# Attention: q and k in two F32R parts, score products of two heads in the two halves of the array

## The reference

```
q, k, v = heads of einsum('btc,fc->btf', layernorm(x), w_qkv)
scores = einsum('bhqd,bhkd->bhqk', q, k) * hs ** -0.5
p = softplus(scores);  p = p * p;  p = p * causal
attn = p / (sum(p) + 1e-9)
x = x + einsum('btc,oc->bto', attn @ v, w_proj) + b_proj
```

## Time and profile before

| | |
|---|---|
| Median of 3 runs | 1591.7 us (1588.0 to 1592.0) |
| The profiled execution | 1588.5 us, its span 1586.4 us |
| Busy: TensorE | 1517.2 us, 96% |
| Busy: VectorE | 1197.2 us, 75% |
| Busy: ScalarE | 872.5 us, 55% |
| qkv phase | about 188 to 275 us of the span |
| attention phase | about 276 to 613 us of the span |
| DMA | mean 60 GB/s |

### The profile page before, as it was taken

The page is one execution under the profiler, slowest core; times in us unless marked ns, Lnnn a source line. Parts: engine busy times, 40 slices in busy tenths (PEclk is TensorE's granted clock), DMA queues, the critical chain, the costliest instruction groups (busy, mean ns, idle before and its releaser), DMA issues. The chain is left out here.

```text
span 1586.4 us, 29112 instructions
## 1 busy us (share of the span) xinstructions
PE 1517.2 (96%) x11188; PEld 1121.0 (71%) x11188; DVE 1197.2 (75%) x2482; ACT 872.5 (55%) x1372; POOL 354.0 (22%) x366
## 2 busy tenths in 40 slices
PE   8999897999999999999989999989999999899998
PEld 7888776444444446888877777766777777678777
DVE  4555697899989996655588887778777777678786
ACT  3333387999999996332332222288888887321220
POOL 0002111100000004000432222114555554211111
PEclk9999999999999999999999999999999999999999
DMA  4100065777777750000110000023333233100000
GB/s 152 34 1 14 4 190 185 102 108 108 108 102 103 101 73 1 14 1 1 40 34 1 1 1 1 3 68 107 97 107 101 97 101 104 41 14 27 14 27 27
DMA packets 57017, 95.80 MB, mean 60 GB/s; under 512 B 7760, under 2 KB 29488, under 8 KB 56880
## 3 DMA queue, kind: packets, MB, share of 16 engines
q1 hardware_dynamic: 55920, 93.35, 26.3%
q10 hardware_dynamic: 960, 0.59, 0.2%
HBM read 76.88 MB, written 17.04 MB: 59 GB/s over the span
## 5 line engine op out<-in xcount | busy, mean ns | idle before, releaser
L928 DVE SCALAR_TENSOR_TENSOR X<-ps,moe_gsel,X 128x256 f32<-128x256 f32 x512 | 246.1, 483 | 71.3 <-PE ps L48 48.5
L1440 DVE TENSOR_TENSOR att_weights<-att_weights 128x1024 f32<-128x1024 f32 (+1 forms) x240 | 263.7, 1148 | 35.6 <-ACT att_weights L1416 35.5
L1416 ACT ACTIVATE att_weights<-ps 128x1024 f32<-128x1024 f32 (+1 forms) x288 | 263.6, 990 | 27.4 <-PE ps L1349 14.6
L48 PE MATMUL ps<-w_experts_hi,moe_xh 128*128 128x512 f32 x512 | 204.2, 399 | 0.1
L48 PE MATMUL ps<-w_experts_hi,moe_xl 128*128 128x512 f32 x512 | 203.1, 397 | 0.0
L48 PE MATMUL ps<-w_experts_lo,moe_xh 128*128 128x512 f32 x512 | 201.5, 394 | 0.0
L1379 PE MATMUL ps<-att_weights,att_v_ones 64*32 64x64 f32 (+5 forms) x2048 | 157.6, 398 | 0.1
L424 ACT ACTIVATE ffn_gates<-ps,ffn_gate_bias 128x512 f32<-128x512 f32 x72 | 49.6, 689 | 148.2 <-PE ps L48 126.5
L48 PEld LDWEIGHTS ps<-w_experts_hi,moe_xh 128*128 128x128 f32 x512 | 96.1, 188 | 24.5 <-DVE X L928 0.7
L48 PEld LDWEIGHTS ps<-w_experts_lo,moe_xh 128*128 128x128 f32 x512 | 96.1, 188 | 22.2
L48 PEld LDWEIGHTS ps<-w_experts_hi,moe_xl 128*128 128x128 f32 x512 | 96.1, 188 | 20.9
(11 more groups left out here) (281 smaller groups left out, 3548.7 us busy)
## 6 DMA issues: line engine op xcount, KB each, us to landing
ssm_lb<-decays SPq DMA_DIRECT2D x32, 512.0 KB, 4.7
ssm_rise<-decays SPq DMA_DIRECT2D x28, 512.0 KB, 4.0
qk_parts<-qkv_part SPq DMA_DIRECT2D x32, 384.0 KB, 2.8
q_stack<-qk_parts SPq DMA_DIRECT2D x64, 128.0 KB, 4.6
k_stack<-qk_parts SPq DMA_DIRECT2D x64, 128.0 KB, 8.0
att_q_stack<-qk_parts SPq DMA_DIRECT2D x64, 128.0 KB, 4.8
att_k_stack<-qk_parts SPq DMA_DIRECT2D x64, 128.0 KB, 8.3
out<-X SPq DMA_DIRECT2D x7, 512.0 KB, 2.9
```

What stands on the lines that cost most here:

```text
L48: ins = pe.matmul(out, l(k), r(k), start=first and n == 0, stop=last and n == len(passes) - 1)
L928: dve.scalar_tensor_tensor(out=x, in0=ring[:, e // 2, (e % 2) * C:(e % 2 + 1) * C], scalar=gsel[:, s, j, e:e + 1], in1=x, op0=ALU.mult, op ...
L1416: act.activation(Wt[:, u % WU, 0:n], scores(u)[:, 0:n], ACT.Softplus).then_inc(softplus_done, 1)
L1440: dve.tensor_tensor(wt, wt, wt, ALU.mult).then_inc(sq_dve, 1)
```

## The change

q and k are written in two F32R parts (high and remainder), 512 KB a store. The second rounding, the third part and their buffers and semaphores go. A stack now has 64 rows for a head: four copies, all four products of two parts. Even heads of the four lie in the lower 64 rows, odd heads in the upper 64, and the free dimension holds two heads instead of four, in F32R: as many bytes as before, 16 DMAs of 128 KB a set, each row of DRAM now 4 KB. A score product reads 64 rows: the two heads of a unit use the two halves of the array and the two banks. Their order in a unit alternates between the heads, and the mask products of REST units follow in pairs, 64 rows each. An UPPER unit is spread over two banks of 256 columns; its products are plain f32 of 64 x 64 in the four quarters of the array, the mask product is made of four 256-column products. Softplus and square of it read 2 x 256 columns. Which heads share rows in the value step changes with it (`h // 2` for `h % 2`), the number of its products doesn't.

The core of the diff:

```diff
-PARTS = 3
-Q_PART = (0, 0, 0, 1, 1, 1, 2, 2)
-K_PART = (0, 1, 2, 0, 1, 2, 0, 1)
-COPIES = P // HD
-STACKED = [(q_or_k, n) for q_or_k in range(2) for n in range(COPIES)]
+PARTS = 2
+HALF = P // 2
+Q_PART = (0, 0, 1, 1)
+K_PART = (0, 1, 0, 1)
+COPIES = HALF // HD
+STACKED = [(q_or_k, odd, n) for q_or_k in range(2) for odd in range(2) for n in range(COPIES)]
...
-        part = sb("part", [P, HALVES, QK, PARTS, GN], BF16)
-        rest = sb("rest", [P, 2, GN], F32)
+        part = sb("part", [P, HALVES, QK, PARTS, GN], F32R)
...
-                    pe.wait_ge(rest_done, n * QK + u + 1)
+                    pe.wait_ge(part1_done, n * QK + u + 1)
...
-            def second(n, h, u):
-                act.wait_ge(rest_done, RING + n * QK + u + 1)
-                act.activation(part[:, h, u, 1], rest[:, u % 2], ACT.Copy).then_inc(part1_done, 1)
...
-            def third(n, h, u):
-                dve.wait_ge(part1_done, n * QK + u + 1)
-                dve.tensor_tensor(part[:, h, u, 2], rest[:, u % 2], part[:, h, u, 1], ALU.subtract).then_inc(part2_done, 1)
...
-                dve.wait_ge(part2_done, 1 + n * QK + max(0, u - 1))
-                dve.scalar_tensor_tensor(out=rest[:, u % 2], in0=ring[:, u], scalar=SCALE[u],
-                                         in1=part[:, h, u, 0], op0=ALU.mult, op1=ALU.subtract).then_inc(rest_done, 1)
+                dve.scalar_tensor_tensor(out=part[:, h, u, 1], in0=ring[:, u], scalar=SCALE[u],
+                                         in1=f32(part[:, h, u, 0]), op0=ALU.mult, op1=ALU.subtract).then_inc(part1_done, 1)
...
-                sp.wait_ge(part2_done, 1 + (i * HALVES + h) * QK + u + 1)
+                sp.wait_ge(part1_done, RING + (i * HALVES + h) * QK + u + 1)
...
-        eng.dma_start(stacks[q_or_k][s][n * HD:(n + 1) * HD],
-                      src.rearrange("(h d) t -> d h t", h=HG)).then_inc(loaded[s], 16)
+        at = odd * HALF + n * HD
+        eng.dma_start(f32(stacks[q_or_k][s][at:at + HD]),
+                      src.rearrange("(g o d) t -> o d g t", o=2, d=HD)[odd]).then_inc(loaded[s], 16)
...
-                pass_units.append([(2 * pair + t, kj, t, c, q, w, part) for t in range(2) for kj, c, q, w, part in together])
+                pass_units.append([(2 * pair + t, kj, t, c, q, w, part) for kj, c, q, w, part in together for t in range(2)])
...
-        uppers = [(h, first + j, 0, (j * 2 + h // 2) * HALF, (first + j) * P, HALF, UPPER) for j in range(GT) for h in range(HG)]
+        uppers = [(h, first + j, h % 2, j * HALF, (first + j) * P, HALF, UPPER) for j in range(GT) for h in range(HG)]
...
-                    for r in range(2):
-                        pe.matmul(scores(u)[r * HALF:(r + 1) * HALF, 0].rearrange("p (s q) -> p s q", q=HALF), neg[low, low],
-                                  ident16[low, low].unsqueeze(1).broadcast_to([HALF, BANK // HALF, HALF]), start=True, stop=False)
+                    for pair in range(2):
+                        for odd in range(2):
+                            own = halves[odd]
+                            pe.matmul(scores(u)[halves[pair], odd, 0:GT * HALF].rearrange("p (j q) -> p j q", q=HALF), neg[own, own],
+                                      ident16[own, own].unsqueeze(1).broadcast_to([HALF, GT, HALF]), start=True, stop=False)
...
-                    ins = pe.matmul(scores(u)[rows, t, c:c + w], SK[s][:, h, keys], SQ[s][:, h, q:q + w],
-                                    start=not upper, stop=n >= len(segments) - 2 if upper else part == FULL)
-                    if part == REST:
-                        ins = pe.matmul(scores(u)[:, t, c:c + HALF], neg[:, :], ident16[:, HALF:P], start=False, stop=True)
+                    own = halves[h % 2]
+                    if upper:
+                        ins = pe.matmul(scores(u)[halves[h // 2], t, c:c + w], f32(SK[s][own, h // 2, kj * P:kj * P + HALF]),
+                                        f32(SQ[s][own, h // 2, q:q + w]), start=False, stop=n >= len(segments) - HG)
+                        continue
+                    ins = pe.matmul(scores(u)[:, t, c:c + w], SK[s][own, h // 2, kj * P:(kj + 1) * P], SQ[s][own, h // 2, q:q + w],
+                                    start=True, stop=part == FULL)
+                    if part == REST and h % 2:
+                        for odd in range(2):
+                            own = halves[odd]
+                            ins = pe.matmul(scores(u)[:, odd, c:c + HALF], neg[own, P:2 * P], ident16[own, own], start=False, stop=True)
...
-                act.activation(Wt[:, u % WU, 0:n], scores(u)[:, 0:n], ACT.Softplus).then_inc(softplus_done, 1)
+                act.activation(Wt[:, u % WU, :, 0:w], scores(u)[:, :, 0:w], ACT.Softplus).then_inc(softplus_done, 1)
```

More of the change, by code:

```diff
@@ L1142, in step @@
                     norm.act_apply(act, n + 2, h, lambda j: tile_of(n + 2, j))
-                for u in range(QK - 2, QK):
-                    second(n, h, u)
                 if left >= 3:
@@ L1188, in step @@
                     tail.dve_add(dve, n + 3, 1 - h)
-                for u in range(QK - 2, QK):
-                    third(n, h, u)
-            dve.sem_inc(rest_done, RING)
-            dve.sem_inc(part2_done, 1)
+            dve.sem_inc(part1_done, RING)
             for h in range(HALVES):
@@ L1271, in attention_phase @@
         at = len(pass_units)
[L1272 removed]
+        uppers = [(h, first + j, h % 2, j * HALF, (first + j) * P, HALF, UPPER) for j in range(GT) for h in range(HG)]
         pass_units.append(uppers)
         pass_steps.append((qb, at, [(h, kj, at, t, c, q, w, part) for h, kj, t, c, q, w, part in uppers]))
[L1275 removed]
+    WIDTH = [BANK // 2 if unit[0][-1] == UPPER else BANK for unit in pass_units]
     PU, PS = len(pass_units), len(pass_steps)
@@ L1376, in value_step @@
                     q0 = q - qb * BANK
-                    rows = slice(h % 2 * HALF, (h % 2 + 1) * HALF) if part == UPPER else slice(0, P)
-                    values = va_up[rows, s, kj, h // 2] if part == UPPER and h % 2 else va[rows, s, kj, h]
+                    rows = halves[h // 2] if part == UPPER else slice(0, P)
+                    values = va_up[rows, s, kj, h % 2] if part == UPPER and h // 2 else va[rows, s, kj, h]
                     ins = pe.matmul(O(qb)[h * 2 * HD:(h + 1) * 2 * HD, q0:q0 + w], values,
@@ L2329, in build @@
                 assert not jobs
-                stacks = [[sides.enter_context(nc.sbuf_tensor(f"{x}_stack{n}", [P, HG, T], BF16, side="right"))] for x in "qk"]
+                stacks = [[sides.enter_context(nc.sbuf_tensor(f"{x}_stack{n}", [P, HG // 2, T], F32R, side="right"))] for x in "qk"]
                 loaded = [nc.alloc_semaphore(name=f"loaded{n}_{s}") for s in range(2)]
@@ L2363, in layout @@
     cols = lambda v: np.ascontiguousarray(v.reshape(-1, P).T)
+    masks = np.triu(np.full((P, P), -1e30, np.float32), 1)
     return {
@@ L2377, in layout @@
         "proj_b": d["L0_attn_b_proj"],
-        "masks": np.triu(np.full((P, P), -1e30, np.float32), 1),
+        "masks": np.concatenate([masks, np.tile(masks[P // 2:], (2, 1))], axis=1),
         "ssm_w": _rows(d["L1_attn_in_proj_w"].T),
```

33 lines of the change are left out of this document (12 added, 21 removed).

## The result

The changed kernel takes 1572.4 us (median of 4 runs, 1569.8 to 1573.1) against 1590.5 for the kernel before in the same job: a ratio of 0.989, 95% interval 0.988 to 0.990. Its profiled execution is 1572.0 us with a span of 1569.9. That is a gain of 18 us where 38 were forecast; it lies inside the range, between rivals B and D.

The account below looks back on a forecast made before the run. TensorE was taken to bound attention and VectorE the qkv stage; 1588.5 less 7 (qkv) and 29 (attention, 1.8 in each of 16 passes) gave 1552.5, stated as 1554 us beside the median, range 1543 to 1582.

Parts of the forecast that it names:

- rival B: Attention: TensorE still binds through loads in turn, slow narrow F32R or dear upper units; 1561 to 1570 us, chance 0.25.
- rival D: Attention: value steps wait on VectorE's lag where it squares all eight units; 1570 to 1586 us, chance 0.11.
- What bounds the kernel: TensorE sets the attention pass of 20.63 us; VectorE sets the qkv step of 10.84 us.
- qkv: qkv stage: removed copies and subtractions shorten a step to 9.5 us, saving 7 us in all; bounds 4 and 10.
- The loop over VectorE: qkv stage: residual, statistics, remainders, add and tanh, put at 8.8 us a step after the change.
- Do the halves overlap: Score products: the two 64-row halves of the array run together, so a full unit costs one product's time.
- C: Score units: the two row halves run one after the other, so the kernel gets slower; 1628 us, chance 0.11.
- Triangle units: Attention's triangle (REST) score units: 1.6 us a pass saved, bounds 0 and 2.1, taking F32R loads as mostly hidden.
- Full units: Attention's full score units: eight products at 0.238 us plus four switches, 2.3 instead of 3.9, 1.6 saved a pass.
- UPPER and transposes: UPPER units go from 0.70 to 0.75 us, 0.1 lost a pass; the transposes' extra switches cost 0.2 a pass.
- What is late next: Attention: ScalarE becomes the bound at 18.4 us a pass, plus 0.4 for its waits on score units: 18.8.
- the forecast's own case: Attention, case A: halves run together and ScalarE binds at 18.8 us a pass; 1548 to 1559 us, chance 0.53.

Follow-up runs that it names:

- The experiment: Changed kernel with a ScalarE copy and a VectorE subtraction of the old sizes put back into each qkv unit, results unread: 1579.2 us, ratio 0.993.
- late masks: Changed kernel with the four mask products of each triangle unit moved behind all its score products: 1561.0 us, ratio 0.982.
- bf16 halves: Changed kernel with the two parts, DRAM buffer and stacks in bf16 instead of F32R, upper products in bf16 too: 1545.2 us, ratio 0.972.
- heads in turn: Changed kernel with both products and masks of one head before the other head's in a triangle unit: 1573.8 us, ratio 0.990.
- F32R masks: Changed kernel with triangle units' mask products in F32R instead of bf16: 1577.5 us in the usual order, 1574.6 with masks behind all score products.
- the kernel without masks: Changed kernel without the mask products of the triangle units, run twice: 1577.4 us, then 1573.2 us.
- the early division: VectorE's division one unit earlier: kernel before 1588.9 us; changed kernel 1569.2 us; with masks behind all score products too, 1559.9 us.

## Why the prediction was right or wrong

**What bounds the kernel: right.** TensorE set the pass before, VectorE the qkv stage. The division, which could have been a hidden second bound of the pass before, cost nothing there (20.62 for 20.63).

**qkv: right in kind, some 2 us too small.** 7 us were forecast, with bounds 4 and 10. From its first product to its last the stage takes 74.7 us instead of 82.6, and with the 1.4 of the earlier last store that is 9.3. The experiment's 6.9 comes so near to the forecast because it leaves that store early. The step fell to 9.3 instead of 9.5, TensorE's floor, and stands there without an idle row. The loop over VectorE, put at 8.8, didn't bind.

**Do the halves overlap: right, and C is out.** Pairs start together, whatever the order of the heads.

**Triangle units: the step that failed most.** The term was 1.6 us a pass with bounds 0 and 2.1. By starts, the eight units with their switches take 4.59 us after the change (four single ones 0.60 each, two pairs 1.09) for 4.94 before: 0.35. The forecast took the upper half of the bounds because the loads of the value products, 16 in 1.01 us, hide altogether. That was the wrong row: those loads stand among products of 320 to 512 columns, while here every second F32R load of a unit stands behind a 64-column one, and the unit's first behind another shape or a mask. No row in front showed an F32R load behind a short product; the nearest price, at most 0.118 a load from the v products, had been worked out and set aside. The unit's two bare loads cost 0.10 (0.51 less the 0.41 of late masks) and 0.12 (0.41 less the 0.29 of bf16), near that bound: 0.29 and 0.22 are the 0.51 measured. The two loads of a pair run beside each other (both at 469.52), which is why it is not the 0.59 of loads in turn. The Trainium skill's rule that was weighed against the change (TensorE: Matmul & The Clock Gate, section on weight-path perf modes: the fast weight load needs a type other than FP32) came out right in effect: with bf16 weights and the same products in the same order, the unit takes 0.29.

**Full units: the second one.** The term was 1.6 saved; it is 0.84 (3.04 us for the eight units, four singly at 0.43 and two pairs at 0.66, for 3.88 before). The product itself is 0.23 as forecast (0.66 less 0.43), but each group of score units starts with a bare F32R load, six of them a pass, which the forecast counted at nothing. A single unit with its switch takes 0.44 here (459.27 to 459.71) and 0.32 with bf16 weights (442.44 to 442.76 in that kernel).

**UPPER and transposes: right.** 0.70 for 0.75, and 0.3 a pass for the switches of the transposes instead of 0.2.

**What is late next: wrong in kind.** 0.4 us a pass was left for ScalarE's ring. The pass got 0.42 on VectorE's division instead, rival D's kind of wait at a place that D didn't name; that the two figures agree is chance. In sum: 20.63 - 0.35 - 0.84 + 0.26 for the transposes + 0.42 = 20.12, and the other groups are 0.04 shorter; measured 20.08. TensorE's own work is then 19.7, the upper end of rival B (whose sum, 20.7 - 1.6 + 0.6, gives 19.7 and not the 19.9 that it states); B's time was too early by the wait.

**The sum.** Of the 16.5 us between the two profiled executions 9.8 are gained up to attention's first score product (0.4 of them in front of the qkv stage) and 7.4 in attention, less 0.7 behind. The forecast had 7 and 29: it failed in attention, and the 2 us more from qkv, which hide a little of that, are luck. The price of the forecast's own case was good: where the loads are fast (bf16 halves), ScalarE binds, with VectorE as full as it, and the pass of 18.63 and the time of 1545 stand beside 18.8 and 1548 to 1559. ScalarE's work is 18.5 us there for the counted 18.4, so nearly nothing of the 0.4 for waits was needed. What was mis-sized was the chance and the term of the F32R load, not the mechanism.

## What to carry to other kernels

Before counting a product by its columns, write down for each weight load the product that stands in front of it: behind 320 columns or more of the same shape an F32R load cost nothing here, behind 64 columns or at a change of shape it cost about 0.1 us, and moving the short products to the end of their group gave back 11 us without changing the work. To split the array's rows between two heads paid in full here only with weights that load fast (bf16); the type chosen to save a part may cost more in loads than the part did. And where an engine has been the bound everywhere, look at each wait that its work has hidden: it is the first thing that a shorter engine meets, and it may be worth nothing again after the next edit.

## What the runs showed of the hardware that was not expected

- The products of the two row halves overlap even when four of one half stand in front of the other's in the stream (heads in turn).
- A change of type between neighbouring products costs nothing that can be seen: F32R masks start like bf16 ones, 0.31 behind the unit's start in the usual order and 0.03 behind the 64-column score products in the late one.
- A wait of TensorE is paid again at the lower clock. Busy time in the second run of the kernel without masks, around a stall of 3.33 us that ends at 433.44:

```profile
429.00:433.00 4.00, 0.95 (x7) 0.15 (x7) 3.90 (x5) 2.60 (x3) 2.79 (x2) 0.99 1.05 130
433.00:437.00 4.00, 3.56 (x17) 1.66 (x17) 0.55 (x3) 1.02 (x1) 0.00 (x0) 0.50 1.05 131
437.00:441.00 4.00, 4.00 (x60) 1.79 (x62) 1.90 (x3) 2.29 (x3) 0.00 (x0) 0.65 0.29 37
```

TensorE has nothing from 430.1 to 433.4; then the granted clock is 0.50 and 0.65, the 1.2 GHz level for most of 8 us, and some 3 us of work are lost again. The pass takes 25.5 us: 19.08, the stall of 3.3 and as much once more.
- Those stalls, which no semaphore ends, came up in several of these kernels: 6 of over 0.5 us in the first run without masks, 5 in the second, one of 2.3 us with F32R masks and one of 0.9 with late ones, two of 1.1 with late bf16 masks, two of 0.9 and 1.2 with heads in turn, one of 1.1 in the changed kernel. The kernel before has none, but with the early division it has one of 0.65, so the new stacks are not needed for one. The five of over 3 us in the two runs without masks come about 64 us apart and begin while a set of stack loads is on its way. For the stall that ends at 440.73 in the first run the loads were issued here (timeline of the queue):

```profile
428.92 3.57 SPq L1229 DMA_DIRECT2D att_q_stack<-qk_parts  x8
432.53 3.69 SPq L1229 DMA_DIRECT2D att_k_stack<-qk_parts  x8
```

and the DMA queues in the half microsecond from 437.0, where the stall begins at 437.4, hold one packet of instructions among loads that fill the 16 engines:

```profile
q1 hardware_dynamic: 27, 0.06, 88.4%
q8 instruction: 1, 0.02, 21.3%
```

That TensorE ran out of instructions because their packet was behind the stack loads fits both, and the kernel with bf16 halves, with half the bytes, has no such stall in attention. No run tested it alone: the cause stays open.
